# Latent cross-attention in a two-layer decoder: score products in row halves, softmax denominators through transfers, output weights split ahead of the loop

## The chip, the cores and the metric

One Trainium2 chip, one of its cores. The metric is the device time of one execution in microseconds (us); the kernel before takes 1911.01 us (median of three runs, 1903.14 to 1913.05). An engine is named as the profile names it: PE is the matrix engine (PEld its weight loads), DVE the vector engine, ACT the scalar engine, POOL the general engine, SP the engine that issues most transfers.

## The reference

The program is a two-layer decoder on x of 32 x 56 x 256. Each layer is self-attention, cross-attention against a context of 32 x 1500 x 64, and a mixture of experts. The change touches the cross-attention of layer 0 alone (the "latent" phase). Cut to what is computed there, with A and Bs the per-head products of the weight matrices:

```python
xn = (x - mean(x)) / sqrt(var(x) + 1e-5)
for b in range(32):                             # batches
    K = rotate(ctx[b])                          # 1500 x 64, ctx*cos + half_swapped(ctx)*sin
    for h in range(16):                         # heads
        q = xn[b] @ A[h]                        # 56 x 64
        p = exp(q @ K.T)                        # 56 x 1500
        c[h] = (p @ K) / p.sum(-1)              # 56 x 64
    x[b] += sum(c[h] @ Bs[h] for h in range(16))
```

There is no maximum taken off before the exponential. Instead the kernel tests that all reciprocals of the denominators lie between 1e-20 and 1e20; a general path, not taken here, stands behind that test.

## The kernel before

The latent phase has three parts: `queries_of` makes q of all batches (64 x 896 per batch, kept as two fp16 tensors: the rounded values and the remainder); then a loop over the 32 batches, which is nearly half of the kernel; then the output product with the weights B16, which are Bs split into fp16 value and remainder.

In the loop the 1500 context rows of a batch stand as 12 tiles of 125 rows (`KT`, `KP`), and the columns as two halves `u` of 448 (8 heads x 56 queries). The six **pairs** of tiles of a batch follow each other; for a pair and both `u`:

- PE makes the scores. The transposed keys `kT` hold for each tile 128 rows: 64 of the rounded keys and 64 of the remainder (the even tile has the rounded ones on top, the odd tile below). A product over all 128 rows with `QH` (the rounded queries, in both row halves) gives two of the three terms at once (L2454); the third, rounded keys times `QL`, takes 64 rows, so the two tiles of a pair use the upper and lower half of the array (L2460).
- ACT takes the exponential of the pair's scores for one `u` (`Pb`, L2537).
- PE multiplies the probabilities of the pair before by the rows `kv` (L2415: 64 output columns each, `u` in one half of the array's columns each).
- DVE adds the tiles of probabilities up (`dsum`, L2600 and L2603, 11 additions per batch, numbered `tt` 1 to 11).

After pair 1 of the next batch, PE sums `dsum` over its partitions with a matrix of ones, so that the denominators of all 448 columns stand in each of 64 rows (L2426). DVE takes their reciprocal on 128 x 448 (`rD`, L2576), updates the test (`good`, L2581 and L2584) and multiplies the values by it (L2589, into `CT`), in the places behind `tt` 4 to 7.

Beside this, the keys of the coming batches are prepared. SP loads the raw rows of batch b (L2320); POOL rotates them in four operations (L2356 to L2364); ACT rounds them to fp16 (`high`, L2509, **in the batch before, between pair 0 and pair 1**) and copies them to `kv` (`rows`, L2515, after pair 1); POOL makes the remainder (L2370); PE transposes `kk` in two turns after pairs 2 and 4 (L2402), and ACT copies each turn out of its bank (`evacuate`, L2500). Each engine runs its instructions in the written order and waits at semaphores. SP's order per step b is: wait until POOL has rotated batch b-2, load rows b, wait until the scores of batch b-2 are done, spread queries b (four transfers, L2334). Buffers are double: raw rows, `kk`, `kT`, `kv`, `QH`, `QL`.

After the loop ACT and POOL make B16 (L2550, L2377).

## Time and profile before

| | |
|---|---|
| runs | 1903.14, 1911.01, 1913.05 us |
| median | 1911.01 us |
| span of the profiled execution | 1905.6 us |
| PE busy in the span | 1505.3 us |
| DVE busy | 1418.2 us |
| ACT busy | 1058.1 us |
| POOL busy | 638.9 us |
| the loop over the batches in the span | about 371 to 1008 us |

The span is what the instructions of the one profiled execution cover; the median of the runs is 5.4 us more. The span holds six phases one after the other, so shares of the whole say little about the one that is changed. The loop is to be read in a window of its own: one batch there is 19.81 us, and all engines repeat with that step. The waits printed beside a row are the idle time of its engine just before it, with what ended it.

### The profile page before, as it was taken

The numbers are of one execution on the slowest core, as the hardware profiler recorded it, in microseconds if no ns is written. First come the engines' busy times: TensorE is split into PE (matmuls) and PEld (weight loads), VectorE is DVE, ScalarE is ACT, GpSimd is POOL, SyncE is SP. The second block draws the span as 40 slices with busy tenths as digits, with TensorE's granted clock in tenths as the row PEclk, the third lists the DMA queues.
The fourth block names the chain that finished last, engine by engine and source line by source line (L and its number), as shares of the span: only waits on it lengthen the run. The fifth ranks groups of instructions, "written<-read, shape, count | busy, mean of one in ns | idle before, by whom it ended". The sixth has DMA issues, their size and how long they took to land. (4 is left out here: it accounts for less than half of the span.)

```text
span 1905.6 us, 37670 instructions
## 1 busy us (share of the span) xinstructions
PE 1505.3 (79%) x12653; PEld 910.4 (48%) x12668; DVE 1418.2 (74%) x2445; ACT 1058.1 (56%) x1759; POOL 638.9 (34%) x653
## 2 busy tenths in 40 slices
PE   1777776999999999999996746880687859956792
PEld 0455553433333333333334635870466537735682
DVE  6888865789898999989986774435688736667574
ACT  1777754766666666666663333440567535536461
POOL 1222211244545545455420234551233210026242
PEclk9665656999999999999997767995799879968897
DMA  6920000112111121111200144434000010023334
GB/s 163 333 87 1 1 1 33 28 36 50 39 40 48 35 51 37 43 46 35 53 11 2 32 121 134 133 110 133 1 2 0 0 25 1 0 86 125 103 107 155
DMA packets 79003, 116.28 MB, mean 61 GB/s; under 512 B 12530, under 2 KB 59834, under 8 KB 78484
## 3 DMA queue, kind: packets, MB, share of 16 engines
q1 hardware_dynamic: 69011, 91.53, 17.0%
q0 software_dynamic: 7776, 21.28, 3.2%
q10 hardware_dynamic: 2112, 2.10, 0.3%
q8 instruction: 65, 1.06, 0.2%
q14 instruction: 39, 0.31, 0.1%
HBM read 59.74 MB, written 40.19 MB: 52 GB/s over the span
## 5 line engine op out<-in xcount | busy, mean ns | idle before, releaser
L2603 DVE TENSOR_TENSOR lat_dsum<-lat_dsum,lat_Pb 125x896 f32<-125x896 f32 x320 | 414.8, 1296 | 62.2 <-ACT lat_Pb L2537 56.1
L2537 ACT ACTIVATE lat_Pb<-banks 125x896 f32<-125x896 f32 x384 | 331.4, 915 | 175.7 <-PE banks L2460 175.0
L2415 PE MATMUL banks<-lat_Pb,lat_kv 125*64 125x448 f32 x1536 | 332.5, 554 | 0.0
L2454 PE MATMUL banks<-lat_QH,lat_kT 128*125 128x448 f16 x768 | 184.5, 363 | 2.7 <-DVE lat_QT L2561 1.9
L2370 POOL TENSOR_TENSOR lat_kk<-lat_rot,lat_kk 125x768 f16<-125x768 f32 x32 | 71.6, 2237 | 317.5 <-ACT lat_kk L2509 317.5
L2415 PEld LDWEIGHTS banks<-lat_Pb,lat_kv 125*64 125x64 f32 x1536 | 93.4, 136 | 154.2 <-issue 153.0
L2454 PEld LDWEIGHTS banks<-lat_QH,lat_kT 128*125 128x125 f16 x768 | 89.7, 137 | 114.8 <-ACT lat_Pb L2537 89.1
L2917 POOL DMA_INDIRECT sent_outputs<-moe_yb,moe_yidx x98 | 99.0, 1010 | 135.4 <-ACT moe_yb L3174 108.4
L3055 PE MATMUL banks<-moe_w2d,moe_gT 88*128 (+3 forms) x780 | 103.9, 285 | 18.7 <-DVE moe_gT L3392 10.0
L2460 PE MATMUL banks<-lat_QL,lat_kT 64*125 64x448 f16 x768 | 114.2, 376 | 0.0
L3380 DVE COPY moe_xTb<-banks 128x1024 f16<-128x1024 f16 x49 | 33.7, 689 | 92.0 <-PE banks L3022 59.7
L2576 DVE RECIPROCAL lat_rD<-banks 128x448 f32<-128x448 f32 x32 | 94.2, 2945 | 1.9 <-PE banks L2426 1.9
L3055 PEld LDWEIGHTS banks<-moe_w2d,moe_gT 88*128 88x128 f16 (+1 forms) x780 | 77.3, 102 | 34.6 <-issue 17.0
L2356 POOL TENSOR_TENSOR lat_rot<-lat_raw,lat_cosK 125x768 f32<-125x768 f32 x32 | 73.5, 2297 | 48.6 <-DMA lat_raw<-in_ctx_dram 45.1
L2909 POOL DMA_INDIRECT sent_rows<-moe_arena,moe_idx x64 | 71.0, 1109 | 52.9 <-DVE moe_idx L3321 33.8
L2972 PE MATMUL banks<-moe_xTb,moe_w2i 128*88 128x256 f16 (+1 forms) x588 | 76.6, 281 | 13.4 <-DVE moe_xTb L3380 13.4
L2972 PEld LDWEIGHTS banks<-moe_xTb,moe_w2i 128*88 (+1 forms) x588 | 63.0, 114 | 20.2 <-issue 15.6
L2500 ACT ACTIVATE lat_kT<-banks 128x1000 f16<-128x1000 f16 x64 | 51.1, 798 | 31.9 <-PE banks L2402 31.8
L2460 PEld LDWEIGHTS banks<-lat_QL,lat_kT 64*125 64x125 f16 x768 | 36.7, 131 | 63.9 <-issue 63.9
L1270 POOL TENSOR_TENSOR bit_vv<-bit_vf,bit_one 128x256 f16<-128x256 f32 x16 | 11.5, 722 | 164.8 <-PE banks L1557 154.3
L3133 ACT ACTIVATE moe_gT<-banks 88x512 f32<-88x512 f32 x37 | 21.9, 591 | 73.3 <-PE banks L2972 49.6
L2364 POOL TENSOR_TENSOR lat_rot<-lat_rot 125x768 f32<-125x768 f32 x32 | 58.8, 1838 | 2.5
(440 smaller groups left out, 3291.2 us busy)
## 6 DMA issues: line engine op xcount, KB each, us to landing
moe_xb<-sent_rows SPq DMA_DIRECT2D x49, 257.0 KB
lat_raw<-in_ctx_dram SPq DMA_DIRECT2D x32, 375.0 KB
sent_rows<-zero SPq DMA_DIRECT2D x1, 7453.0 KB, 47.9
lat_QH<-lat_QT SPq DMA_DIRECT2D x64, 112.0 KB, 2.2
lat_QL<-lat_QT SPq DMA_DIRECT2D x64, 112.0 KB, 2.2
moe_arena<-sent_outputs SPq DMA_DIRECT2D x12, 512.0 KB, 6.5
sent_rows<-zero SPq DMA_DIRECT2D x1, 5140.0 KB, 64.4
sent_outputs<-zero SPq DMA_DIRECT2D x1, 4096.0 KB, 39.4
```

Of the source, the lines that this page charges most:

```text
L2356: s(nc.gpsimd.tensor_tensor(rot[:, par], r, cosK[:], ALU.mult))
L2370: nc.gpsimd.tensor_tensor(halves(par, True), paired(rot[:, par]), halves(par, False), ALU.subtract).then_inc(kl_made, 1)
L2415: ins = nc.tensor.matmul(ps[u * DC:(u + 1) * DC, 4 + par, 0:8 * T], kv[:, par, tt, :], Pb[:, tt % NPB, u, :], start=tt == 0, stop=tt == KT ...
L2454: nc.tensor.matmul(ps[0:KP, 2 * u + tt % 2, 0:8 * T], kT[:, par, tt, 0:KP], queries(QH, u), start=True, stop=False)
L2460: ins = nc.tensor.matmul(ps[0:KP, 2 * u + tt % 2, 0:8 * T], kT[rows, par, tt, 0:KP], queries(QL, u, rows), start=False, stop=True)
L2537: nc.scalar.activation(Pb[:, slot:slot + 2, u, :], ps[0:KP, 2 * u:2 * u + 2, 0:8 * T], ACT.Exp, scale=1.0 / QSCALE).then_inc(exp_done, 1)
L2576: s(nc.vector.reciprocal(rD[:], ps[:, 7, 0:8 * T]))
L2603: ins = nc.vector.tensor_tensor(dsum[:, par], dsum[:, par], Pb[:, tt % NPB], ALU.add)
L2909: nc.gpsimd.indirect_dma_start(xg[:, :], bass.IndirectOffsetOnAxis(ap=idx[:, c, i:i + 1], axis=0), rows[:, i, :], None).then_inc((sent0, s ...
L2917: nc.gpsimd.indirect_dma_start(ytok[:, :], bass.IndirectOffsetOnAxis(ap=yidx[:, n, h:h + 1], axis=0), yb[:, n % 3, h, :], None).then_inc(y ...
L2972: ins = nc.tensor.matmul(ps[0:FP, dst, j * BN:(j + 1) * BN], w[:, u, c, j * FP:(j + 1) * FP], rhs(v, c), start=a + c == 0, stop=a == 2 and ...
L3055: ins = nc.tensor.matmul(dst, gT2[:, n % 2, u, j, h * P:(h + 1) * P], w[:, v, j, :], start=a + j == 0, stop=last and not (gated and b < 0))
```

## The change

Three edits, all in the latent phase.

1. **Scores.** `kk` now holds, per pair, one tile of 128 columns with the rounded keys of both tiles and one with both remainders. All three terms of the scores are products over 64 rows, the even tile in the upper and the odd tile in the lower half of the array. The order is now all terms of `u` 0, then all of `u` 1; before, the two `u` were interleaved.
2. **Denominators.** ACT copies the denominators (128 x 448) from the bank to `den`, inside pair 2 between its two exponentials. SP spreads one row of each half over 64 partitions x 7 elements (`den7`, two transfers), DVE takes the reciprocal of 128 x 7 behind `tt` 7, SP writes that to a buffer in device memory, waits for it, and loads it back broadcast to `rD` (two transfers). DVE multiplies behind `tt` 10. The test on the reciprocals moves behind the loop. The last batch keeps the old way.
3. **Output weights.** Both operations on B16 run on POOL, at the start of the block.

```diff
             def halves(par, low):
-                units = kk[:, par].rearrange("p (a q) u d -> p a (q u) d", q=2)
-                return units[:, :, 1:3, :] if low else units[:, :, 0:4:3, :]
+                return kk[:, par, low:KT:2, :]
...
                     def body(b, par):        # SP
                         ...
+                        if past(b, 2):
+                            spread_reciprocals(b - 2)
+
+                    def spread_reciprocals(b):
+                        sp.wait_ge(den_kept, b + 1)
+                        for u in range(2):
+                            sp.dma_start(den7[u * DC:(u + 1) * DC, :],
+                                         den[u * DC:u * DC + 1, :].rearrange("o (p e) -> o p e", e=DR)
+                                         ).then_inc(den_in, 16)
+                        sp.wait_ge(rec_made, b + 1)
+                        sp.dma_start(recs.rearrange("u (p e) -> (u p) e", e=DR),
+                                     rec7[:, ds(b, 1), :].rearrange("p o e -> p (o e)")
+                                     ).then_inc(rec_sent, 16)
+                        sp.wait_ge(rec_sent, 16 * b + 16)
+                        if past(b, 1):
+                            sp.wait_ge(ct_made, b)
+                        for u in range(2):
+                            sp.dma_start(rD[u * DC:(u + 1) * DC, :],
+                                         recs[u:u + 1, :].broadcast_to([DC, 8 * T])
+                                         ).then_inc(rec_in, 16)
...
                 def _(pool):
                     s = Steps(pool, own_pool)
+                    nc.gpsimd.tensor_copy(B16[:, :, 0, :], Bs[:]).then_inc(bh_made, 1)
+                    pool.wait_ge(bh_made, 1)
+                    nc.gpsimd.tensor_tensor(B16[:, :, 1, :], Bs[:], B16[:, :, 0, :],
+                                            ALU.subtract).then_inc(bl_made, 1)
...
-                            pe.wait_ge(ct_made, b)
+                            pe.wait_ge(den_kept, b)
...
-                                for tt in both:
-                                    nc.tensor.matmul(ps[0:KP, 2 * u + tt % 2, 0:8 * T],
-                                                     kT[:, par, tt, 0:KP], queries(QH, u),
-                                                     start=True, stop=False)
-                            for u in range(2):
-                                for tt in both:
-                                    rows = slice(0, DC) if tt % 2 == 0 else slice(DC, P)
-                                    ins = nc.tensor.matmul(ps[0:KP, 2 * u + tt % 2, 0:8 * T],
-                                                           kT[rows, par, tt, 0:KP],
-                                                           queries(QL, u, rows),
-                                                           start=False, stop=True)
+                                for n, (low, Q) in enumerate(((0, QH), (0, QL), (1, QH))):
+                                    for q in range(2):
+                                        rows = slice(q * DC, (q + 1) * DC)
+                                        ins = nc.tensor.matmul(ps[0:KP, 2 * u + q, 0:8 * T],
+                                                               kT[rows, par, 2 * pair + low, 0:KP],
+                                                               queries(Q, u, rows),
+                                                               start=n == 0, stop=n == 2)
...
+                    def keep_denominators(b):        # ACT, called inside pair 2
+                        act.wait_ge(den_done, b + 1)
+                        if past(b, 1):
+                            act.wait_ge(den_in, 32 * b)
+                        nc.scalar.activation(den[:], ps[:, 7, 0:8 * T], ACT.Copy).then_inc(den_kept, 1)
...
-                    nc.scalar.activation(B16[:, :, 0, :], Bs[:], ACT.Copy).then_inc(bh_made, 1)
...
-                            s(nc.vector.reciprocal(rD[:], ps[:, 7, 0:8 * T]))
+                        nc.vector.reciprocal(rec7[:, ds(b, 1), :].rearrange("p o e -> p (o e)"),
+                                             den7[:]).then_inc(rec_made, 1)
...
-                            if tt in range(4, 8) and past(b, 1):
-                                attended(b - 1, (par + 1) % 2, tt - 4)
+                            if tt == 7 and past(b, 1):
+                                reciprocals(b - 1)
+                            if tt == KT - 2 and past(b, 1):
+                                dve.wait_ge(rec_in, 32 * b)
+                                context(b - 1, (par + 1) % 2)
```

On SP, one step of the loop and the start of the next. Before (`lat_raw` are the raw rows, `lat_QH` and `lat_QL` the spread queries; ISA and REGISTER_ALU rows prepare addresses and carry waits):

```order
L2320 ISA [waits lat_rows_rotated]
L2320 DMA lat_raw<-in_ctx_dram 125x768
L2329 REGISTER_ALU [waits lat_ql_made]
L2334 ISA [waits lat_scores_done]
L2334 DMA lat_QH<-lat_QT 64x896 x2
L2334 ISA
L2334 DMA lat_QL<-lat_QT 64x896 x2
L2320 ISA [waits lat_rows_rotated]
L2320 DMA lat_raw<-in_ctx_dram 125x768
```

The same step in the changed kernel, up to the next step's load of raw rows:

```order
L2341 DMA lat_QL<-lat_QT 64x896 x2
L2352 DMA lat_den<-lat_den 64x1x7 [waits lat_den_kept]
L2352 DMA lat_den<-lat_den 64x1x7
L2356 ISA [waits lat_reciprocals_made]
L2356 DMA lat_reciprocals<-lat_rec 128x7
L2359 ISA
L2363 DMA lat_rD<-lat_reciprocals 64x448 [waits lat_ct_made,lat_reciprocals_sent]
L2363 DMA lat_rD<-lat_reciprocals 64x448
L2327 ISA [waits lat_rows_rotated]
L2327 DMA lat_raw<-in_ctx_dram 125x768
```

The load of the next raw rows (last row) stood directly behind the spread of the queries; it now stands behind five transfers and the waits in front of them.

On PE, a pair of tiles without a turn. Before:

```order
L2415 MATMUL banks<-lat_Pb,lat_kv 64x448 x4
L2454 MATMUL banks<-lat_QH,lat_kT 125x448 x4
L2460 MATMUL banks<-lat_QL,lat_kT 125x448 x4
L2415 MATMUL banks<-lat_Pb,lat_kv 64x448 x4
L2402 MATMUL banks<-id,lat_kk 128x125 x4
```

and in the changed kernel:

```order
L2484 MATMUL banks<-lat_QH,lat_kT 125x448 x2
L2484 MATMUL banks<-lat_QL,lat_kT 125x448 x2
L2484 MATMUL banks<-lat_QH,lat_kT 125x448 x4
L2484 MATMUL banks<-lat_QL,lat_kT 125x448 x2
L2484 MATMUL banks<-lat_QH,lat_kT 125x448 x2
L2437 REGISTER_ALU
L2444 MATMUL banks<-lat_Pb,lat_kv 64x448 x4
```

Four products over 128 rows and four over 64 became twelve over 64, in the order `QH`, `QL`, `QH` for each `u`.

On DVE, the additions of batch 1 before, with the work on batch 0's denominators between them:

```order
L2603 TENSOR_TENSOR lat_dsum<-lat_dsum,lat_Pb 125x896 [waits lat_summed,lat_exp_done] x3
L2576 RECIPROCAL lat_rD<-banks 128x448 [waits lat_denominators_done]
L2603 TENSOR_TENSOR lat_dsum<-lat_dsum,lat_Pb 125x896 [waits lat_summed,lat_exp_done]
L2581 SCALAR_TENSOR_TENSOR lat_good<-lat_rD,lat_good 128x448 [waits lat_dve]
L2603 TENSOR_TENSOR lat_dsum<-lat_dsum,lat_Pb 125x896 [waits lat_summed,lat_exp_done]
L2584 SCALAR_TENSOR_TENSOR lat_good<-lat_rD,lat_good 128x448 [waits lat_dve]
L2603 TENSOR_TENSOR lat_dsum<-lat_dsum,lat_Pb 125x896 [waits lat_summed,lat_exp_done]
L2589 TENSOR_TENSOR lat_QT<-banks,lat_rD 128x448 [waits lat_pv_done,lat_dve]
```

and in the changed kernel:

```order
L2618 TENSOR_TENSOR lat_dsum<-lat_Pb 125x896 [waits lat_exp_done]
L2621 TENSOR_TENSOR lat_dsum<-lat_dsum,lat_Pb 125x896 [waits lat_summed,lat_exp_done] x6
L2602 RECIPROCAL lat_rec<-lat_den 128x7 [waits lat_den_spread]
L2621 TENSOR_TENSOR lat_dsum<-lat_dsum,lat_Pb 125x896 [waits lat_summed,lat_exp_done] x3
L2607 TENSOR_TENSOR lat_QT<-banks,lat_rD 128x448 [waits lat_pv_done,lat_reciprocals_loaded]
L2621 TENSOR_TENSOR lat_dsum<-lat_dsum,lat_Pb 125x896 [waits lat_summed,lat_exp_done]
```

The reciprocal moved from behind `tt` 4 to behind `tt` 7 and shrank to 7 columns; the multiplication moved from behind `tt` 7 to behind `tt` 10 and waits for a transfer.

## Rows read from the trace of the kernel before

**Rows 1.** The page, part 1: busy time of the engines over the whole span.
```profile
PE 1505.3 (79%) x12653; PEld 910.4 (48%) x12668; DVE 1418.2 (74%) x2445; ACT 1058.1 (56%) x1759; POOL 638.9 (34%) x653
```

**Rows 2.** Windows view of one batch: stretch, length, busy per engine, granted clock, DMA.
```profile
709.30:729.11 19.81, 19.81 (x114) 7.72 (x113) 18.14 (x16) 13.42 (x17) 9.83 (x5) 1.00 0.16 43
```

**Rows 3.** Timeline of PE in that batch: start, us, engine, line, names, form.
```profile
709.30 0.97 PE L2454 MATMUL banks<-lat_QH,lat_kT 128*125 128x448 f16 x4
710.21 0.59 PE L2460 MATMUL banks<-lat_QL,lat_kT 64*125 64x448 f16 x4
710.73 1.72 PE L2415 MATMUL banks<-lat_Pb,lat_kv 125*64 125x448 f32 x8
712.38 0.97 PE L2454 MATMUL banks<-lat_QH,lat_kT 128*125 128x448 f16 x4
...
719.29 0.61 PE L2402 MATMUL banks<-id,lat_kk 125*128 125x125 f16 x8
719.74 0.92 PE L2454 MATMUL banks<-lat_QH,lat_kT 128*125 128x448 f16 x4
```

**Rows 4.** Timeline of ACT in that batch.
```profile
710.81 1.73 ACT L2537 ACTIVATE lat_Pb<-banks 125x896 f32<-125x896 f32 x2 [1.43 <-PE banks L2460]
712.42 0.84 ACT L2509 ACTIVATE lat_kk<-lat_rot 125x768 f16<-125x768 f32 x1
713.88 1.73 ACT L2537 ACTIVATE lat_Pb<-banks 125x896 f32<-125x896 f32 x2 [0.62 <-PE banks L2460]
715.49 0.84 ACT L2515 ACTIVATE lat_kv<-lat_rot 125x768 f32<-125x768 f32 x1
...
719.94 1.01 ACT L2500 ACTIVATE lat_kT<-banks 128x1000 f16<-128x1000 f16 x1 [0.66 <-PE banks L2402]
```

**Rows 5.** Timeline of SP's transfers there: the end of one step, the next load.
```profile
709.13 1.15 SPq L2334 DMA_DIRECT2D lat_QL<-lat_QT  x2
710.48 0.33 SPq L2320 DMA_DIRECT2D lat_raw<-in_ctx_dram  x1
```

**Rows 6.** Timeline of POOL: the first and last rotation step and the remainder.
```profile
716.20 2.30 POOL L2356 TENSOR_TENSOR lat_rot<-lat_raw,lat_cosK 125x768 f32<-125x768 f32 x1 [0.45 <-DMA lat_raw<-in_ctx_dram]
...
722.19 1.81 POOL L2364 TENSOR_TENSOR lat_rot<-lat_rot 125x768 f32<-125x768 f32 x1
733.29 2.27 POOL L2370 TENSOR_TENSOR lat_kk<-lat_rot,lat_kk 125x768 f16<-125x768 f32 x1 [9.29 <-ACT lat_kk L2509]
```

**Rows 7.** Timeline of POOL ahead of the loop: the same rotation, DVE nearly idle.
```profile
323.78 1.81 POOL L2356 TENSOR_TENSOR lat_rot<-lat_raw,lat_cosK 125x768 f32<-125x768 f32 x1 [34.95 <-DMA lat_raw<-in_ctx_dram]
...
327.81 1.81 POOL L2364 TENSOR_TENSOR lat_rot<-lat_rot 125x768 f32<-125x768 f32 x1
```

**Rows 8.** Timeline of DVE in the loop: additions and the reciprocal.
```profile
708.79 4.45 DVE L2603 TENSOR_TENSOR lat_dsum<-lat_dsum,lat_Pb 125x896 f32<-125x896 f32 x4
...
721.18 2.94 DVE L2576 RECIPROCAL lat_rD<-banks 128x448 f32<-128x448 f32 x1
```

**Rows 9.** DMA view: issues by line, count, KB each, median us from issue to landing.
```profile
lat_QH<-lat_QT SPq DMA_DIRECT2D x64, 112.0 KB, 2.2
...
hmask<-in_hmask_dram SPq DMA_DIRECT2D x1, 4.0 KB, 1.6
...
rot_bv<-in_rot_bqkv_dram SPq DMA_DIRECT2D x1, 1.0 KB, 4.2
```

**Rows 10.** Timeline of PE at the start of the loop, just after it had waited.
```profile
373.43 1.82 PE L2454 MATMUL banks<-lat_QH,lat_kT 128*125 128x448 f16 x4 [0.82 <-ACT lat_Pb L2537]
...
379.30 1.14 PE L2454 MATMUL banks<-lat_QH,lat_kT 128*125 128x448 f16 x4
```

**Rows 11.** Timeline of the loop's end: POOL's split, an addition, PE's denominators.
```profile
1007.71 4.68 POOL L2377 TENSOR_TENSOR lat_B<-lat_Bs,lat_B 128x2048 f16<-128x2048 f32 x1 [34.45 <-ACT lat_B L2550]
1008.51 4.83 DVE L2603 TENSOR_TENSOR lat_dsum<-lat_dsum,lat_Pb 125x896 f32<-125x896 f32 x1
...
1013.39 1.76 PE L2426 MATMUL banks<-lat_dsum,lat_ones 125*64 125x448 f32 x4 [5.78 <-DVE lat_dsum L2603]
```

More of the change, by code:

```diff
@@ L2294, in latent_attention @@
             rD = sb("rD", [P, 8 * T], c=main)
+            DR = 8 * T // DC
+            den = sb("den", [P, 8 * T], c=main)
+            den7, rec7 = sb("den7", [P, DR], c=main), sb("rec7", [P, B - 1, DR], c=main)
+            recs = nc.dram_tensor("lat_reciprocals", (2, 8 * T), F32, kind="Internal").ap()
+            den_kept, den_in, rec_made, rec_sent, rec_in = (
+                sem("den_kept"), sem("den_spread"), sem("reciprocals_made"), sem("reciprocals_sent"),
+                sem("reciprocals_loaded"))
             good, all_good = sb("good", [P, 8 * T], c=main), sb("all_good", [P, 1], c=main)
-            badf = sb("badf", [1, 1], c=main)
+            badf, good7 = sb("badf", [1, 1], c=main), sb("good7", [P, 1], c=main)
             ones = sb("ones", [KP, DC], c=main)
@@ L2439, in body, with queries @@
                             return
-                        def queries(Q, u, rows=slice(0, P)):
+                        def queries(Q, u, rows):
                             return Q[rows, par, 8 * u:8 * u + 8, :].rearrange("p h t -> p (h t)")
                         for pair in range(KT // 2):
-                            both = (2 * pair, 2 * pair + 1)
                             for u in range(2):
@@ L2539, in body @@
                                                      ACT.Exp, scale=1.0 / QSCALE).then_inc(exp_done, 1)
+                                if pair == 2 and u == 0 and past(b, 1):
+                                    keep_denominators(b - 1)
                             if live(b + 1, B):
```

58 lines of the change are left out of this document (31 added, 27 removed).

## The prediction

> **What bounds the kernel now.** I read the engines' shares first [rows 1]: PE 79%, DVE 74% of the span. They are averages over six phases, so the second view is a window of one batch of the loop [rows 2]: PE is busy 19.81 of 19.81 us at granted clock 1.00 (2.4 GHz), DVE 18.14, ACT 13.42, POOL 9.83. PE is the bound, without a gap. DVE stands close behind.
>
> The third view is PE's timeline in that batch [rows 3]. One pair of tiles is the distance from 709.30 to 712.38: 3.08 us. The four `QH` products begin 0.91 us before the `QL` ones, these 0.52 us before the values, and the values take 1.65 us. Here is how I split it: the records overlap, so I go by starts. If one 448-column product streams for x, the `QH` stage holds 4x plus a change of array layout, the `QL` stage 2x (two tiles at once, one in each half of the rows) plus a change. 0.91 - 0.52 = 2x gives x = 0.19 us, and about 0.14 us for a change. After a turn the first products start with no such gap: the eight transposes at 719.29 are followed by `QH` at 719.74, both being full-height layouts.
>
> The fourth view is who feeds whom. ACT rounds the keys of the next batch (L2509) in pair 0 [rows 4]; POOL then waited 9.29 us for ACT [rows 6]. So the rotated rows lie ready long before they are wanted: the rotation ends at 722.19 + 1.81 = 724.0, and ACT asks for them one batch after 712.42, at 732.2. **The slack of the raw rows is 8.2 us.** It exists because SP issues their load at 710.48, right after the queries [rows 5].
>
> **Part 1, scores.** Before a pair has three changes of layout (`QH` to `QL`, `QL` to values, values to `QH`). After, two. In the two pairs with a turn, the full-height transposes stand between values and scores: three before, three after. So four changes of 0.14 us go per batch: 0.6 us. The streamed columns are the same, 12 products of 64 rows in six concurrent pairs for 4 + 2 streams. PE's batch would be 19.2 us. ACT gains slack, since `u` 0 is complete after 0.56 us of a pair.
>
> The Trainium skill, "TensorEngine Tiling (Array Packing)", Key Properties, says that a switch of tiling mode drains the array; it names no price, and the 0.14 us here are the trace's.
>
> **Part 2, denominators.** DVE loses the 2.94 us reciprocal [rows 8] and two small operations, gains one of 7 columns (by 2.94 x 7/448 about 0.05 us and a start, 0.1 us). DVE is not the bound, so this frees nothing by itself. ACT gains a copy of 128 x 448: 0.5 us beside 13.42, hidden.
>
> The cost lies in SP's queue. The load of rows b+1 now stands behind the denominators' transfers, whose middle one waits for DVE's reciprocal, behind `tt` 7, behind the exponentials of pair 3. Before, the load was issued about 1.2 us into a batch; after, past two thirds of it. That is more than the slack of 8.2 us, so ACT stops at L2509 in pair 0 until POOL has rotated. Behind ACT's wait are queued all exponentials from pair 1 on; for them wait PE (scores of pair 2) and DVE, and for DVE, by way of `tt` 7, SP's next load. **It is a ring, and its length is the new time of a batch.** I walk it from the start of L2509 in one batch to its start in the next.
>
> a) ACT: L2509, two exponentials of pair 1, L2515 and the first of pair 2. By starts [rows 4] a pair of exponentials is 1.61, L2509 and L2515 about 0.72 each: first exponential of pair 1 ended at 1.6, all begun by 3.1, then the copy to `den` and the second one: 5.1 us.
> b) PE meanwhile: it has done everything up to pair 2 during the stop. Scores of pair 2 from 1.65, values, the turn. At full clock 1.12 + 0.14 + 1.65 + 0.45: turn done at about 5.2. But PE has then waited some 6 us (the ring's length less its own work), and it resumes at half clock. The trace shows this at the loop's start [rows 10]: after a gap of 0.82 us and others before it four `QH` products took 1.82 us instead of 0.97, and at 379.30 they took 1.14: the pace came back there, some 6.5 us later. At the end of the loop, after 5.78 us of idle time, the four denominator products took 1.76 us [rows 11]. At half clock: turn done at 8.4.
> c) ACT copies the turn (1.01, of which 0.9 before the next can start) and makes both exponentials of pair 3 (1.73): 11.1 us (8.1 at full clock).
> d) DVE adds `tt` 6 and 7, 1.1 each [rows 8]: 13.3. The spread of `den` was issued from 4.5 on and has landed.
> e) Reciprocal and hand-over to SP: 13.5.
> f) Transfer to memory and its wait. No row shows a write of 28-byte pieces to memory. Nearest are 2.2 us for the spread of the queries; the ends are 1.6 and 4.2 [rows 9]. I take 2.2, the most similar in issuer and layout: 15.7.
> g) Two broadcast issues at 0.57 us (half of a pair's 1.15 [rows 5]) and 0.2 to the load: 17.1.
> h) The load lands 5.5 us after issue (710.48 to 716.20, less 0.2 for the hand-overs) [rows 5, 6]: 22.6.
> i) POOL rotates: 7.8 us in the loop (716.20 to 724.0) [rows 6], 5.84 ahead of it (323.78 to 329.62) while DVE idles [rows 7]. By then DVE has run out of exponentials, so 5.84: **28.5 us**.
>
> The Trainium skill, "DMA: Bandwidth & Descriptors", Anatomy of one DMA, gives a fixed 2.0 us per transfer, most of it the receipt of the write, memory being the slowest target; with it step f would be 0.2 us shorter and the result 6 us lower. Its Specifications say that below 512 bytes a transfer does read-modify-write; no row here shows what that costs.
>
> The first load that moves is that of batch 3, the last that of batch 31: 29 intervals between starts of L2509. 29 x (28.5 - 19.81) = +252 us. The other three batches gain 0.6 each: -1.8.
>
> The broadcast that DVE awaits behind `tt` 10 lands about 5.2 us after the reciprocal; the additions 8 to 10 depend on exponentials of pairs 4 and 5, 4 to 5 us later. DVE may wait about 1 us, and has 4 us to spare per batch: nothing, except in the last batch (1 us).
>
> **Part 3, output weights.** At the loop's end POOL's 4.68 us subtraction held one addition for 4.83 us instead of 1.1, while PE waited 5.78 us [rows 11]. With this gone, and DVE no longer behind: -4.5, the upper bound being the 5.78. Ahead of the loop the two operations take some 9 us before the first rotation at 323.78 (which waited 34.95 us for its data [rows 7]); they end about 4 us after that, and POOL waits for ACT until 334 anyway. 0 to +3 us for POOL beside DVE; I take +1.
>
> **Sum.** 252 - 1.8 - 4.5 + 1 = +247, on the span of 1905.6: 2152.6. The median of the runs lies 5.4 above that span: **2158 us**.
>
> **Rivals.**
> 1. *PE keeps its full clock through the stop.* Steps b and c end 3.0 us earlier, the ring is 25.5: 29 x 5.7 - 5 = +160, 2071 us. For it: the stop is only a fifth of a batch. Against: both rows after such a wait show half clock. An end between (back after half the time) is likely enough to count here.
> 2. *The clock is low for more of the batch, or the rotation takes the full 7.8 us.* With i) at 7.8 the ring is 30.5, with the 4.2 us write as well 32.5: 2216 to 2274. If PE stayed at 1.2 GHz for all of it, its work would be 38 us a batch and bound: 1911 + 29 x 18.6 = 2450; against it, a PE that never waits was granted 1.00 [rows 2]. The Trainium skill, "TensorE: Matmul & The Clock Gate", Part 1, on oscillation, describes a loop that waits for its data in every round and starts each round at the half rate; [rows 10, 11] agree for a single wait. Taken alone it gives the 28.5 above.
> 3. *Faster: the load is not late.* If the load's shift stayed within the 8.2 us, there would be no ring, and the changes of layout decide: 32 x 0.6 + 4.5 - 1 = 23 us less, 1888 us. It needs the reciprocal within 5.7 us of a batch's start (1.2 + 8.2, less the 3.6 of steps f and g). But in the trace of before, ACT's copy of the turn, which stands ahead of pair 3's exponentials, begins 10.6 us into the batch (719.94 against 709.30) [rows 3, 4], and the reciprocal follows those exponentials by two additions. It would hold if SP did not wait in written order.
> 4. *Full-height rate lost:* 64-row products do not overlap, 12 x 0.19 instead of 6: PE's batch 19.2 + 6.7 = 26. The `QL` products speak against it (four in 0.52 us), and in the ring it would still be covered: no time of its own, up to 2180.
>
> **Chances.** The ring as summed, 27 to 30 us: 0.55. Rival 1 with its intermediate values: 0.20. Rival 2: 0.15, of which 0.02 for the low clock throughout. Rival 3: 0.08. Something that leaves the time as it is (a shift that lands just past the slack): 0.02. The range from 2065 to 2245 takes in most of the first three. A measurement here tells about 0.5% apart, 9.5 us: faster 0.08, same 0.02, slower 0.90.
>
> **What would show it.** In the profile after: ACT's L2509 (its new line) idle before it by 7 to 10 us, ended by POOL's rotation; POOL's first rotation step waiting for `lat_raw` by over 15 us; SP's load of raw rows issued some 17 us after L2509's start; steps of 27 to 30 us between them, 29 times; a granted clock below 1.00 in parts of the loop; the PE window no longer full. A pair without turn of 2.92 us at full clock shows part 1. Wrong would be: the load issued before the reciprocal's transfers, or L2509 without a wait.

## The result and the profile after

The changed kernel takes **2130.21 us** (median of 2126.03 to 2134.0) against 1910.2 us before, run beside it: 1.1158 times as long, 95% interval 1.1133 to 1.1183. The prediction was 2158 us, range 2065 to 2245. The span of the profiled execution is 2124.3 us, 218.7 us more than before.

The page of the changed kernel: busy time by engine, then the rotation's first step on POOL and the rounding of the keys on ACT (line, names, shapes, count, busy, mean ns, idle before).

```profile
PE 1527.5 (72%) x13421; PEld 940.8 (44%) x13436; DVE 1248.2 (59%) x2385; ACT 1065.1 (50%) x1789; POOL 563.7 (27%) x654
...
L2389 POOL TENSOR_TENSOR lat_rot<-lat_raw,lat_cosK 125x768 f32<-125x768 f32 x32 | 58.5, 1828 | 556.7 <-DMA lat_raw<-in_ctx_dram 556.3
L2533 ACT ACTIVATE lat_kk<-lat_rot 125x768 f16<-125x768 f32 x32 | 27.0, 842 | 258.4 <-POOL lat_rot L2397 258.4
```

Every engine has lost share against [rows 1], PE among them, although PE still is the busiest. The waits view from 420 to 1200 us, all of it in the loop (engine and line, what it waits for, us in total, times, longest) name two links of the ring, and PE, which hangs on it:

```profile
POOL lat_rot L2389 <- DMA lat_raw<-in_ctx_dram: 536.3, 28, 20.7
...
ACT lat_kk L2533 <- POOL lat_rot L2397: 249.3, 28, 9.5
PE banks L2484 <- ACT lat_Pb L2567: 192.1, 29, 7.2
```

One batch of the loop, as [rows 2] (stretch, length, busy PE, PEld, DVE, ACT, POOL, granted clock, DMA):

```profile
726.60:753.93 27.33, 21.06 (x136) 8.94 (x136) 12.64 (x13) 13.68 (x17) 7.23 (x5) 0.87 0.16 40
```

PE is busy for 21.06 of 27.33 us and the granted clock is 0.87, where it had 19.81 of 19.81 at 1.00. In the same stretch ACT's timeline (start, us, engine, line, names; in brackets the idle time before), the answer to [rows 4]:

```profile
726.60 0.84 ACT L2533 ACTIVATE lat_kk<-lat_rot 125x768 f16<-125x768 f32 x1 [8.71 <-POOL lat_rot L2397]
...
733.65 1.01 ACT L2524 ACTIVATE lat_kT<-banks 128x1000 f16<-128x1000 f16 x1 [1.77 <-PE banks L2431]
734.55 1.72 ACT L2567 ACTIVATE lat_Pb<-banks 125x896 f32<-125x896 f32 x2
...
753.93 0.84 ACT L2533 ACTIVATE lat_kk<-lat_rot 125x768 f16<-125x768 f32 x1 [8.55 <-POOL lat_rot L2397]
```

PE's timeline, for [rows 3]:

```profile
728.30 0.64 PE L2484 MATMUL banks<-lat_QH,lat_kT 64*125 64x448 f16 x2 [6.43 <-ACT lat_Pb L2567]
...
730.73 2.34 PE L2444 MATMUL banks<-lat_Pb,lat_kv 125*64 125x448 f32 x8
733.00 0.61 PE L2431 MATMUL banks<-id,lat_kk 125*128 125x125 f16 x8
...
734.83 1.72 PE L2444 MATMUL banks<-lat_Pb,lat_kv 125*64 125x448 f32 x8
```

DVE's addition of `tt` 6 and 7 and its new reciprocal:

```profile
736.40 2.22 DVE L2621 TENSOR_TENSOR lat_dsum<-lat_dsum,lat_Pb 125x896 f32<-125x896 f32 x2 [2.18 <-ACT lat_Pb L2567]
738.53 0.19 DVE L2602 RECIPROCAL lat_rec<-lat_den 128x7 f32 x1
```

SP's transfers, where [rows 5] had the load right behind the queries:

```profile
738.86 0.36 SPq L2356 DMA_DIRECT2D lat_reciprocals<-lat_rec  x1
740.33 1.10 SPq L2363 DMA_DIRECT2D lat_rD<-lat_reciprocals  x2
741.64 0.32 SPq L2327 DMA_DIRECT2D lat_raw<-in_ctx_dram  x1
```

And POOL's rotation, for [rows 6]:

```profile
748.00 1.82 POOL L2389 TENSOR_TENSOR lat_rot<-lat_raw,lat_cosK 125x768 f32<-125x768 f32 x1 [18.69 <-DMA lat_raw<-in_ctx_dram]
...
752.02 1.80 POOL L2397 TENSOR_TENSOR lat_rot<-lat_rot 125x768 f32<-125x768 f32 x1
```

The whole ring stands in these rows: keys rounded (726.60), exponentials, turn (733.00), exponentials of pair 3 (from 734.55), additions, reciprocal (738.53), its way to memory and back, load (741.64), landing (748.00), rotation to 753.82, keys rounded (753.93).

To set kernels side by side, the span is cut in four: up to the start of ACT's rounding in step 2 of the loop; 29 steps of that start; from the last one to the result of the test on the reciprocals; the rest, which no edit touches. All in us, from one profiled execution each.

| kernel | to step 2 | mean step | tail | rest | span |
|---|---|---|---|---|---|
| before | 395.3 | 19.81 | 51.0 | 884.8 | 1905.6 |
| after | 389.9 | 27.78 | 45.1 | 883.9 | 2124.3 |
| part 1 alone | 393.5 | 21.32 | 51.3 | 867.7 | 1930.8 |
| parts 1 and 3 | 390.6 | 21.25 | 48.5 | 864.2 | 1919.7 |
| part 3 alone | 395.3 | 19.81 | 46.5 | 862.8 | 1878.9 |
| after, load first | 392.3 | 20.00 | 45.1 | 868.1 | 1885.5 |
| after, load in the middle | 391.4 | 20.16 | 42.3 | 862.8 | 1881.0 |
| before, load late | 400.4 | 27.00 | 51.8 | 863.4 | 2098.6 |
| after, PE kept busy | 394.6 | 26.54 | 48.7 | 868.8 | 2081.9 |
| load first, reciprocal behind `tt` 5 | 392.7 | 19.23 | 44.0 | 888.6 | 1883.0 |
| part 1 without the test operations | 392.1 | 19.23 | 49.3 | 887.0 | 1886.0 |
| part 1, short rotation | 392.3 | 19.23 | 50.2 | 879.3 | 1879.4 |

The rest differs by some 20 us for equal work from one set of runs to the next (the kernel before took 1884 us beside experiments 1 to 6 and 12, 1905 us beside 7 and 9 to 11, 1903 us beside 8). It isn't tied to the chip: one and the same chip gave 1884 and 1903 us. So times are compared as ratios to the kernel before in the same set. The loop's step doesn't follow: 19.81 in "before" and in "part 3 alone". The mean of "after, PE kept busy" holds one early step of 34.94 us; the median there is 26.13, and 27.72 in "after".

### The profile page after: what moved, and what is told of

It reads as the page before. It is cut to its first block and busy times, and to the rows that moved or that the text cites. A ratio compares the mean times of both kernels' runs of the same rounds, so it can differ in the third digit from the quotient of the medians.

```text
span 2124.3 us, 39474 instructions
## 1 busy us (share of the span) xinstructions
PE 1527.5 (72%) x13421; PEld 940.8 (44%) x13436; DVE 1248.2 (59%) x2385; ACT 1065.1 (50%) x1789; POOL 563.7 (27%) x654
## 5 line engine op out<-in xcount | busy, mean ns | idle before, releaser
L2621 DVE TENSOR_TENSOR lat_dsum<-lat_dsum,lat_Pb 125x896 f32<-125x896 f32 x320 | 353.1, 1103 | 438.9 <-ACT lat_Pb L2567 433.4
L2484 PE MATMUL banks<-lat_QH,lat_kT 64*125 64x448 f16 x1536 | 275.2, 397 | 194.6 <-ACT lat_Pb L2567 192.7
L2444 PE MATMUL banks<-lat_Pb,lat_kv 125*64 125x448 f32 x1536 | 351.3, 581 | 0.0
L2484 PEld LDWEIGHTS banks<-lat_QH,lat_kT 64*125 64x125 f16 x1536 | 113.7, 145 | 332.4 <-ACT lat_Pb L2567 281.3
L2389 POOL TENSOR_TENSOR lat_rot<-lat_raw,lat_cosK 125x768 f32<-125x768 f32 x32 | 58.5, 1828 | 556.7 <-DMA lat_raw<-in_ctx_dram 556.3
L2444 PEld LDWEIGHTS banks<-lat_Pb,lat_kv 125*64 125x64 f32 x1536 | 98.7, 145 | 174.0 <-issue 154.0
L2533 ACT ACTIVATE lat_kk<-lat_rot 125x768 f16<-125x768 f32 x32 | 27.0, 842 | 258.4 <-POOL lat_rot L2397 258.4
L2484 PE MATMUL banks<-lat_QL,lat_kT 64*125 64x448 f16 x768 | 149.0, 384 | 0.0
L2403 POOL TENSOR_TENSOR lat_kk<-lat_rot,lat_kk 125x768 f16<-125x768 f32 x32 | 52.7, 1648 | 78.1 <-ACT lat_kk L2533 78.1
L2484 PEld LDWEIGHTS banks<-lat_QL,lat_kT 64*125 64x125 f16 x768 | 58.0, 148 | 12.9
L1270 POOL TENSOR_TENSOR bit_vv<-bit_vf,bit_one 128x256 f16<-128x256 f32 x16 | 11.5, 717 | 162.6 <-PE banks L1557 152.1
```

Source lines behind the costliest of these rows:

```text
L2389: s(nc.gpsimd.tensor_tensor(rot[:, par], r, cosK[:], ALU.mult))
L2403: nc.gpsimd.tensor_tensor(halves(par, True), paired(rot[:, par]), halves(par, False), ALU.subtract).then_inc(kl_made, 1)
L2444: ins = nc.tensor.matmul(ps[u * DC:(u + 1) * DC, 4 + par, 0:8 * T], kv[:, par, tt, :], Pb[:, tt % NPB, u, :], start=tt == 0, stop=tt == KT ...
L2484: ins = nc.tensor.matmul(ps[0:KP, 2 * u + q, 0:8 * T], kT[rows, par, 2 * pair + low, 0:KP], queries(Q, u, rows), start=n == 0, stop=n == 2)
L2621: ins = nc.vector.tensor_tensor(dsum[:, par], dsum[:, par], Pb[:, tt % NPB], ALU.add)
```

## The experiments

Two theories stood at the start. **Ring**: the late load of the raw rows costs everything, the rest of the change is worth a small gain. The rival: the detour of the denominators itself (transfers, DVE's wait for them) or the new form of the scores costs a good part.

**1. The load of raw rows ahead of the denominators' transfers** (the five transfers that stood at the end of a step now stand behind the next step's load; nothing else moved).

```diff
                             sp.wait_ge(rotated, b - 1)
                             load_rows(b, par)
+                            if past(b, 3):
+                                spread_reciprocals(b - 3)
...
-                        if past(b, 2):
-                            spread_reciprocals(b - 2)
...
```

> The changed kernel, with SP's order altered: the load of raw rows b is issued ahead of the five transfers for the denominators of batch b-3 and of the waits in front of them, so that it comes about 1 us into a batch, as in the kernel before. All else as changed. Theory (the ring through SP's queue): ACT's rounding (L2533) finds its rows ready, the step of a batch falls from 27.8 to PE's own 19.2 us, the time to 2130 - 29 x 8.6 = 1881 us (1875 to 1892). Rival (the transfers themselves, DVE's wait for the broadcast, or the 64-row products cost the time, wherever the load stands): it stays above 2050. Rival (half of it is the wait of DVE behind tt 10): about 2000.

Measured: 1882.04 us, ratio 0.9989 (0.9974 to 1.0003). The order of five issues in one queue is worth 11 to 12% of the kernel. But of the gain that rival 3 had for a load in time (23 us, 1.2%) nothing is left: the step is 20.00 us, not 19.2. That the time lies in the expected 1875 to 1892 us is luck, since the kernel before was some 25 us faster in this set than in the one that the expectation went by. Experiments 9 to 11 return to this.

**2. The load in the middle**, between the spread of the denominators and the wait for the reciprocal.

```diff
...
                         if past(b, 2):
+                            spread_denominators(b - 2)
+                        if past(b, 1) and live(b + 1, B):
+                            sp.wait_ge(rotated, b)
+                            load_rows(b + 1, (par + 1) % 2)
+                        if past(b, 2):
                             spread_reciprocals(b - 2)
...
```

> The changed kernel, with the load of raw rows b+1 issued between the spread of the denominators and the wait for the reciprocal. The load then leaves about 5.9 us after the start of L2533, lands 5.6 us later, POOL rotates in 5.8 to 7.8: a ring of 17.3 to 19.3 us against PE's 19.2. Theory (slack, then ring): the wait of ACT is gone or under 0.5 us, 1880 to 1890 us. Rival (any shift of the load costs its length): the shift is about 8 us against the kernel with the load first, so over 2000 us.

Measured: 1882.81 us, ratio 0.9989 (0.9975 to 1.0002), step 20.16. In the waits view (400 to 900 us) ACT's rounding still waits for POOL in every step, where under 0.5 us was expected, and POOL's timeline shows the rotation:

```profile
ACT lat_kk L2537 <- POOL lat_rot L2401: 70.0, 25, 3.0
```
```profile
725.72 2.74 POOL L2393 TENSOR_TENSOR lat_rot<-lat_raw,lat_cosK 125x768 f32<-125x768 f32 x1 [8.42 <-DMA lat_raw<-in_ctx_dram]
...
732.16 2.54 POOL L2401 TENSOR_TENSOR lat_rot<-lat_rot 125x768 f32<-125x768 f32 x1
```

So here, too, there is a ring, a short one: from one rounding (714.59) to the copy of the denominators that SP waits for, the load (issued at 720.39), the landing (725.72), the rotation beside a working DVE (9.0 us, to 734.70), and the next rounding (734.81), 20.2 us. It is barely longer than PE's own 19.2. What makes the ring long is the wait for the reciprocal (behind `tt` 7).

**3. The kernel before with the late load and nothing else.**

```diff
                             sp.wait_ge(rotated, b - 1)
+                            sp.wait_ge(summed, (b - 2) * (KT - 1) + 7)
                             load_rows(b, par)
```

> The kernel before with one wait more and nothing else: SP issues the load of raw rows b only when DVE has done addition tt 7 of batch b-2. No transfer is added. Theory: the late load alone makes the ring. Its length is that of the changed kernel, 27.3 us, less the transfer to memory and the broadcasts (2.8) and a shorter landing (0.9), plus DVE's long reciprocal and the first test ahead of tt 7 (1.8): about 25 us (24 to 26.5); ACT idle before L2509 by 5 to 8 us; 1910 + 30 x 5.3 = 2069 us (2040 to 2110). Rival (it is the added transfers that cost, not the load's place): 1910 us.

Measured: 2099.7 us (two runs), ratio **1.1143** (1.1112 to 1.1173), step 27.00. The old scores, the old reciprocal and no detour, yet nearly the whole loss: 1.1143 of 1.1158. The step is a miss: 24 to 26.5 us were expected, with a load that lands 0.9 us sooner than in the changed kernel; it took as long (6.3 us), and the turn came later, as the rows below show. The new kernel has a longer ring by the detour (27.78) and gains elsewhere. Timelines of SP, POOL, ACT and PE in this kernel:

```profile
710.59 0.27 SPq L2320 DMA_DIRECT2D lat_raw<-in_ctx_dram  x1
```
```profile
716.88 1.81 POOL L2357 TENSOR_TENSOR lat_rot<-lat_raw,lat_cosK 125x768 f32<-125x768 f32 x1 [17.71 <-DMA lat_raw<-in_ctx_dram]
```
```profile
723.47 0.84 ACT L2510 ACTIVATE lat_kk<-lat_rot 125x768 f16<-125x768 f32 x1 [6.57 <-POOL lat_rot L2365]
...
731.66 1.01 ACT L2501 ACTIVATE lat_kT<-banks 128x1000 f16<-128x1000 f16 x1 [2.34 <-PE banks L2403]
```
```profile
725.17 1.81 PE L2455 MATMUL banks<-lat_QH,lat_kT 128*125 128x448 f16 x4 [4.52 <-ACT lat_Pb L2538]
...
727.85 3.23 PE L2416 MATMUL banks<-lat_Pb,lat_kv 125*64 125x448 f32 x8
...
731.46 0.93 PE L2455 MATMUL banks<-lat_QH,lat_kT 128*125 128x448 f16 x4
```

Here PE, after 4.52 us of waiting, ran at half its clock for some 6 us (values in 3.23 instead of 1.72 us), and the turn was copied 8.2 us after the rounding. In the changed kernel it was 7.05 us.

**4. PE kept busy through the stop.** Added: 34 products ahead of the scores of pair 2, into the bank of the turns; the next turn overwrites them.

```diff
+                                if pair == 2 and u == 0 and past(b, 1):
+                                    for k_ in range(34):
+                                        nc.tensor.matmul(ps[0:KP, 6, 0:8 * T],
+                                                         kT[0:DC, par, 0, 0:KP],
+                                                         queries(QH, 0, slice(0, DC)),
+                                                         start=True, stop=True)
```

> The changed kernel with 34 products of 64 x 448 more on PE per batch, ahead of the scores of pair 2, where it waits 6.4 to 7.2 us; their results go to the bank of the transposes and are overwritten. At full clock they take 6.4 us. Theory: PE keeps 2.4 GHz over the stop, its scores, values and turn after it take 3.5 instead of 5.2 us, the ring shrinks from 27.8 by 1.7 us: 2130 - 49 = 2081 us. Rival (the half clock is hidden behind ACT, or the clock does not react): 2130 us or, if the added products run into the resume, more.

Measured: 2075.75 us, ratio 1.1011 (1.0987 to 1.1036). ACT's timeline:

```profile
720.01 0.84 ACT L2539 ACTIVATE lat_kk<-lat_rot 125x768 f16<-125x768 f32 x1 [8.87 <-POOL lat_rot L2397]
...
725.54 1.01 ACT L2530 ACTIVATE lat_kT<-banks 128x1000 f16<-128x1000 f16 x1 [0.29 <-PE banks L2431]
...
746.06 0.84 ACT L2539 ACTIVATE lat_kk<-lat_rot 125x768 f16<-125x768 f32 x1 [8.80 <-POOL lat_rot L2397]
```

The turn is copied 5.53 us after the rounding, 1.52 earlier than in the changed kernel (7.05), and the step shown is 26.05 against 27.33. The granted clock from 420 to 1160 us is 1.00. PE's work rose by 6.6 us a batch and the kernel got faster by 1.3%: the clock's share of the ring is 1.2 us a step by the means (26.54 against 27.78), 1.6 by the medians; 1.7 were expected, and rival 1 gave it 3.0. With the full clock the ring still costs 10%.

**5. Part 1 alone**: the diff of the change, of which only the hunks on `kk` (`halves`), on PE's scores and on its turns are kept; denominators and weights are the old ones.

> The kernel before with part 1 alone. Theory: four changes of array layout of 0.14 us fewer per batch, a pair without a turn 2.92 to 2.95 us instead of 3.08, 32 x 0.6 = 19 us less: 1891 us. Rival (products of 64 rows in two halves don't overlap, or their weight loads show): the pair becomes longer than 3.08 us and the time over 1930.

Measured: 1923.32 us, ratio **1.0209** (1.0193 to 1.0225), a miss: slower by 2%, not faster. The windows view (600 to 800 us), the view of DVE's groups (500 to 900) and PE's waits (420 to 900) of this kernel:

```profile
600.00:800.00 200.00, 186.13 (x1268) 76.66 (x1264) 198.05 (x140) 124.29 (x151) 99.68 (x48) 0.98 0.16 40
```
```profile
L2597 DVE TENSOR_TENSOR lat_dsum<-lat_dsum,lat_Pb 125x896 f32<-125x896 f32 x186 | 279.0, 1500 | 3.8
...
L2594 DVE TENSOR_TENSOR lat_dsum<-lat_Pb 125x896 f32<-125x896 f32 x19 | 41.5, 2187 | 0.0
```
```profile
PE banks L2425 <- DVE lat_dsum L2597: 28.4, 22, 2.0
```

DVE, third from the left of the busy times, is busy for 198.05 of 200 us and PE waits for its additions. An addition takes 1500 ns on average, where the same view of before has 1306; the first of a batch, which has a row of its own, takes 2187 instead of 1083. DVE's other operations take as long as before.

**6. Parts 1 and 3**: the same with the third edit, B16 made by POOL at the start of its block, added.

> The kernel before with part 1 (scores in row halves) and part 3 (output weights ahead of the loop), and the denominators as before, on DVE. Theory: PE's batch 19.2 instead of 19.8, the loop's end 4.5 us shorter: 1910 - 19 - 4.5 = 1886 us. If DVE, busy 18.1 of 19.8 us before, becomes the bound, the step stays near 19.5 and the time is about 1896. Against the run with the load first it also tells whether the denominators by transfer gain anything: the theory says at most 5 us.

Measured: 1921.69 us, 1.02 (1.018 to 1.0219), a miss again (1886 to 1896 us were expected, beside 1910), step 21.25, DVE 198.05 of 200 us again. Two questions followed: is DVE's amount of work the cause, and what makes an addition long?

**7. Part 1 without the two operations of the test** on the reciprocals (`good`; left out for all batches but the last stages behind the loop).

```diff
-                            if tt in range(4, 8) and past(b, 1):
+                            if tt in (4, 7) and past(b, 1):
                                 attended(b - 1, (par + 1) % 2, tt - 4)
...
```

> The kernel before with the scores in row halves (p1, 1.021) and without the two operations per batch that test the reciprocals (L2575, L2578): that test is left out for all batches but the last. Step of p1: 21.3 us on average, DVE busy 198 of 200 us. Theory: DVE with what POOL takes from it is the bound of p1, so 1.2 us less work on DVE gives at least 1.0 us per batch: ratio 1.005 or less. Rival (DVE's busy time is only waiting that the trace books as work; PE's new order of the two halves is what costs): 1.02 as before.

Measured: 1889.52 us, ratio 0.9911 (0.9883 to 0.9938), step 19.23, PE busy 200 of 200. 1.2 us less on DVE per batch turned 1.0209 into 0.9911, and the additions fell to 1292 ns, too (500 to 900 us).

**8. Part 1 with POOL's rotation cut to its first operation** (the kernel leaves the sine terms out of the keys and so computes something else; DVE's own work is untouched).

```diff
-                        s(nc.gpsimd.tensor_tensor(rot[:, par], r, cosK[:], ALU.mult))
-                        ...
-                        nc.gpsimd.tensor_tensor(rot[:, par], rot[:, par], rot2[:],
-                                                ALU.add).then_inc(rotated, 1)
+                        nc.gpsimd.tensor_tensor(rot[:, par], r, cosK[:], ALU.mult
+                                                ).then_inc(rotated, 1)
```

> Part 1 alone, with POOL's rotation cut to its first operation (the sine terms are left out of the keys). Part 1 alone had a loop step of 21.32 us and a ratio of 1.021, DVE busy 198 of 200 us with additions of 1.50 us mean. Theory C: DVE is over its bound only because POOL's two-input operations and DVE's additions hold each other up. With three of four of them gone, the additions fall to about 1.1 us, DVE needs 11 x 1.1 + 2.94 + 3 x 0.6 = 16.9 us a batch, PE is the bound again at 19.23 us a step: 29 x (19.23 - 19.81) = -17 us, -2 for the first batches, ratio 0.99. Rival D: the order in which DVE's operations stand (reciprocal, tests and product between additions 4 to 7) makes the chain too long by itself, whatever POOL does: additions fall, but the step stays above 20.5 us, ratio 1.01 or more.

Measured: 1884.18 us, ratio 0.9897 (0.9869 to 0.9925), step 19.23. The same two views:

```profile
600.00:800.00 200.00, 200.00 (x1412) 85.85 (x1408) 174.47 (x157) 139.06 (x168) 45.03 (x21) 1.00 0.18 46
```
```profile
L2589 DVE TENSOR_TENSOR lat_dsum<-lat_dsum,lat_Pb 125x896 f32<-125x896 f32 x210 | 247.5, 1179 | 48.1 <-ACT lat_Pb L2523 44.8
```

With POOL's three other operations gone the additions fall from 1500 to 1179 ns and DVE is no longer the bound, at the same list of DVE operations. The cut touches nothing of DVE's own, so what made part 1 slow is DVE and POOL holding each other up, on a DVE that had little to spare: experiment 7 did as much by taking work off DVE. The Trainium skill, "SBUF — State Buffer", Who interferes with whom, has the rule: a DVE instruction with two inputs in SBUF contends with a GpSimd instruction that reads SBUF, and one that starts first blocks the other whole; the means of 1500 and 1179 ns agree, and so does the single addition of 4.83 us beside POOL's operation of 4.68, which ended 0.95 us after that one [rows 11].

**9. Load first, and the reciprocal behind `tt` 5** instead of `tt` 7. Two theories for the lost gain of experiment 1: the multiplication's wait for the broadcast (W), or the collisions with POOL (P).

```diff
-                            if tt == 7 and past(b, 1):
+                            if tt == 5 and past(b, 1):
                                 reciprocals(b - 1)
```

> The kernel with the load first (e1), with DVE's short reciprocal behind tt 5 instead of behind tt 7, so that the broadcast leaves and lands about 4 us sooner. In e1 the step of a batch is 20.0 us, not PE's 19.2. Theory W: DVE's wait for the broadcast behind tt 10 (up to 2.3 us) and PE's waits for DVE behind it make the difference: the wait vanishes, the step falls to 19.3, 20 us less than e1, ratio to before 0.989. Theory P (DVE's additions and POOL's operations, both with two inputs from SBUF, exclude each other; 11 x 1.09 + 7.2 us of POOL alone are 19.2 us of a batch, before any gap): DVE's wait vanishes, the step stays at 19.7 to 20.0 and the ratio between 0.995 and 1.000.

Measured: 1882.26 us beside 1905.24, ratio **0.9872** (0.985 to 0.9893): faster than both kernels, by 1.3% than before and, by the ratios, by 11.5% than the changed one (0.9872 / 1.1158). The windows view of experiment 1's kernel, then of this one:

```profile
600.00:800.00 200.00, 191.62 (x1356) 83.23 (x1356) 170.73 (x130) 135.81 (x168) 97.39 (x50) 1.00 0.20 54
```
```profile
600.00:800.00 200.00, 200.00 (x1412) 86.08 (x1412) 171.18 (x137) 143.32 (x178) 99.51 (x51) 1.00 0.22 58
```

PE is back to 200 of 200 us. The waits of experiment 1's kernel (420 to 900) and its DVE timeline say what stood in the way:

```profile
DVE lat_QT L2607 <- DMA lat_rD<-lat_reciprocals: 40.5, 20, 2.3
...
PE banks L2444 <- DVE lat_QT L2607: 15.6, 16, 1.3
```
```profile
728.62 0.19 DVE L2602 RECIPROCAL lat_rec<-lat_den 128x7 f32 x1
728.73 3.34 DVE L2621 TENSOR_TENSOR lat_dsum<-lat_dsum,lat_Pb 125x896 f32<-125x896 f32 x3
733.85 0.62 DVE L2607 TENSOR_TENSOR lat_QT<-banks,lat_rD 128x448 f32 x1 [1.77 <-DMA lat_rD<-lat_reciprocals]
```

From reciprocal to multiplication there are 5.2 us of transfers and only three additions (3.34 us) to fill them. PE in turn waits for the multiplication before it can make values into the same bank. With five additions between, DVE's wait is gone from its groups, though an addition still takes 1504 ns there.

**10. The same with the multiplication behind `tt` 9.**

```diff
-                            if tt == KT - 2 and past(b, 1):
+                            if tt == KT - 3 and past(b, 1):
                                 dve.wait_ge(rec_in, 32 * b)
```

> As the run with the reciprocal behind tt 5, and DVE's multiplication behind tt 9 instead of tt 10, so that PE's first values of the batch after next (which wait for it) come free 1 to 2 us sooner. Theory W: the same as with tt 10 or 2 us better, 0.988. Theory P: no change against it, 0.995 to 1.000.

Measured: 1882.67 us, 0.9877 (0.9857 to 0.9898), step 19.23: the same as with `tt` 10. Four additions (`tt` 6 to 9) cover the transfers as well.

**11. Load first, reciprocal behind `tt` 7, the rotation cut** as in experiment 8 (sine terms left out).

> The kernel with the load first (e1), with POOL's rotation cut to its first operation: the sine terms are left out of the keys and values, three of POOL's five operations per batch go, about 3.8 us of POOL alone (7 us beside DVE). Theory P: the additions take 1.1 to 1.3 us instead of 1.53 on average, DVE catches up, PE is the bound again, step 19.2 us, ratio 0.986. Theory W: the broadcast comes no earlier relative to tt 7, the step stays at 19.8 or more, 0.997.

Measured: 1882.04 us, 0.9877 (0.9856 to 0.9898), step 19.23, additions 1128 ns instead of 1530. P removes the shortfall as W did. By experiment 9 the long additions (1504 ns) alone do no harm: DVE had no room for them and for a wait of 2 us together. That the wait alone would do none is not shown, since with the short rotation it nearly went as well (7.7 us in 25 times, 0.6 at most, instead of 40.5 in 20).

**12. Part 3 alone**: of the change's diff only the hunks on B16.

> The kernel before with part 3 alone. Theory: the addition that took 4.83 us beside POOL's subtraction takes 1.1, PE's wait of 5.78 us at the loop's end shrinks to about 2: 1906 us, 4 us less (3 to 5). Rival (the two operations ahead of the loop delay the first rotation or DVE by as much): no change.

Measured: 1880.88 us, 0.9976 (0.9966 to 0.9986): 3.5 us less in the median, 4.5 in the tail. PE's wait for the last denominators fell from 5.78 [rows 11] to 2.05 us.

## Why the prediction was right, and where it was off

**The ring and its links were right.** Its length, step by step, from the start of L2533 at 726.60 (rows above):

| step | predicted | measured |
|---|---|---|
| a) ACT through pair 2's exponentials | 5.1 | 5.3 |
| b) turn done | 8.4 | 7.0 |
| c) exponentials of pair 3 | 11.1 | 9.7 |
| d) `tt` 6 and 7 | 13.3 | 12.0 |
| e) reciprocal, handed to SP | 13.5 | 12.3 |
| f) write landed | 15.7 | 13.7 |
| g) load issued | 17.1 | 15.0 |
| h) rows landed | 22.6 | 21.4 |
| i) rotated | 28.5 | 27.2 |

The mean of the 29 steps is 27.78 (26.93 to 29.36), so 29 x (27.78 - 19.81) = +231 instead of +252. Three terms were mis-sized. **Step b**, by 1.4 us: the half clock was taken for the whole way to the turn, by the 6.5 us of [rows 10]; here it lasted about 3.7 us from PE's start at 728.30: the granted clock is 0.50 up to 730.73, 0.72 from there to 733.00 and 1.00 after, and the eight values at 730.73 take 2.34 us, between a full 1.72 and the 3.23 of experiment 3. In experiment 3, the turn's copy came 8.2 us after the rounding, close to step b's figure. Why the clock came back sooner in the one than in the other isn't settled. **Step f**, by 0.7: the write to memory took 1.5 us, under the lower end of 1.6. **Step h**, by 0.9 the other way: 6.4 us from issue to POOL's start instead of 5.5. In this kernel and in experiment 3 (6.3 us) the spread of the queries is issued behind the load, after 0.6 and 1.6 us; before, it came first. The queries' transfers took longer themselves. The DMA view of the changed kernel, for [rows 9] (line, count, KB each, median us to landing):

```profile
lat_QH<-lat_QT SPq DMA_DIRECT2D x64, 112.0 KB, 2.8
lat_QL<-lat_QT SPq DMA_DIRECT2D x64, 112.0 KB, 4.9
...
lat_den<-lat_den SPq DMA_DIRECT2D x62, 1.8 KB, 1.9
lat_reciprocals<-lat_rec SPq DMA_DIRECT2D x31, 3.5 KB, 1.5
```

That load and queries hold each other up is a reading of these rows, and experiment 2 bears it out: with the queries issued 7.7 us behind the load, POOL started 5.4 us after the load's issue (median of the loop; 6.4 in the changed kernel), and the queries landed in 2.3 and 2.2 us. Step i was right to take the undisturbed rotation: 5.82 us against 5.84.

The Trainium skill's price for step f ("DMA: Bandwidth & Descriptors", Anatomy of one DMA, 2.0 us fixed, a fit for transfers that the general engine issues; here SP issued them) would have been 0.5 us too long as well; the measured 1.5 us decides.

Two side sums are off by a little. With the turn done at 5.2, step c at full clock ends at 7.9 and not 8.1, which makes rival 1 a ring of 25.3 us and 2065 us; and rival 3 needed the reciprocal within 5.8 us, not 5.7.

**The other terms.** Of the difference of the spans, +218.7: loop +231, tail -5.9 (predicted -4.5 for part 3 and -1.2 for the two batches that lie there), the stretch up to step 2 -5.4 (predicted about zero), rest -0.9. The 5.4 are for the most part not the change's doing. Half of them lies ahead of every edited instruction: SP issues the first raw rows at 315.50 instead of 318.34. The rest lies between ACT's first and third rounding, 59.1 us instead of 61.8. There PE ran at half clock in the kernel before [rows 10]; part 3 alone has the same instructions on PE, made its first values at full clock (1.73 us) and took 59.3. Ahead of the loop the new operations on B16 delay the first rotation by some 0.6 us (6.0 us from the load's issue instead of 5.4), which costs nothing, since POOL then waits 4.4 us for ACT. POOL's timeline there, for [rows 7]:

```profile
317.50 4.06 POOL L2377 TENSOR_TENSOR lat_B<-lat_Bs,lat_B 128x2048 f16<-128x2048 f32 x1
321.52 1.81 POOL L2389 TENSOR_TENSOR lat_rot<-lat_raw,lat_cosK 125x768 f32<-125x768 f32 x1
```

I had them end 4 us past the first rotation's start; they end with it. At the loop's end PE's wait of 5.78 us [rows 11] became:

```profile
1233.90 0.97 PE L2455 MATMUL banks<-lat_dsum,lat_ones 125*64 125x448 f32 x4 [1.49 <-DVE lat_dsum L2621]
```

**Part 1's price on PE was right.** A pair without a turn goes from values to values in 2.94 us, predicted 2.92, here on PE at full clock:

```profile
707.33 1.72 PE L2444 MATMUL banks<-lat_Pb,lat_kv 125*64 125x448 f32 x8
...
710.27 1.72 PE L2444 MATMUL banks<-lat_Pb,lat_kv 125*64 125x448 f32 x8
```

And wherever PE bounds the loop with the new scores the batch is 19.23 us (experiments 7 to 11), predicted 19.2. Rival 4 is out with that: the 64-row products do overlap.

**One sentence failed: "DVE is not the bound, so this frees nothing by itself."** With PE's batch at 19.2 and DVE at 18.14 [rows 2] it left 1.1 us between them, and counted DVE's busy time as if it stayed. With part 1 alone the additions met POOL's operations more, by their means (the rows show the growth, not why the phase moved): they grew to 1500 ns, and DVE became the bound at 21.3 us. So part 2 does free something: without it part 1 is a loss of 2%, with it and an early load and reciprocal (experiment 9) a gain of 1.3%. In the changed kernel the ring hides this, since DVE idles through the stop (its additions there take 1.1 us). For the same reason rival 3's 1888 us was too simple: a load in time alone gave 0.9989; its 1.2% came only with the wait for the broadcast or the collisions gone. "DVE may wait about 1 us ... nothing" was in that case wrong too: it waited up to 2.3 us, and had no room for it. In the changed kernel itself that wait was 1.8 us at most, off the ring.

**The other marks** that were named for a right ring: ACT's wait ahead of the rounding 8.6 to 8.7 us (7 to 10), POOL's for the rows 18.69 (over 15), clock 0.87 in the step. Rival 1 was half right in mechanism (experiment 4: the clock costs 1.2 to 1.6 us of the ring), rival 2's longer rotation did not come.

## What to carry to other kernels

A prefetch has a slack (here 8.2 us), and an in-order queue spends it for every wait written ahead of the prefetch. Where such a wait hangs, over several engines, on the prefetched data itself, the delay closes into a ring whose length is the new time of the loop; then no engine's total work sets the time, only the pieces that lie on the ring, and moving one issue ahead of the wait gives it all back. Before an engine at 90% is called "not the bound", its busy time is to be split into work and hold-ups, since the same additions took 15% longer here once the order around them changed; and a detour through memory wants enough work written between its start and the instruction that needs it.

## What the runs showed that I had not expected

- Part 1 alone is faster on the bound engine and slower as a whole: additions 1306 ns before, 1500 with part 1, 1179 with the rotation cut, 1091 in the changed kernel whose DVE and POOL rarely meet.
- PE at half clock after waits came back after about 3.7 us in the changed kernel (6.43 us of waiting before) and after about 6 us in experiment 3 (4.52 us of waiting). Adding 6.6 us of products to each batch made the kernel 1.3% faster.
- A write of 128 pieces of 28 bytes to memory landed in 1.5 us, less than the 1.9 us of the spread of 1.8 KB inside the core.
- A load of 375 KB took 5.4 to 5.5 us with nothing behind it, and 6.3 to 6.4 with 448 KB of transfers issued 0.6 to 1.6 us behind.
